# Four graph layers on one core: a ring of 1024 instead of 16384 bytes for Pool's DMA descriptors

## The reference

```python
h = jnp.maximum(_layernorm(x, axis=-1), 0.0)
x = x + _L0_gnn_ref(h, edge_attr_32, src, dst)       # mean of h[src] * pattern, plus h
h = jnp.maximum(_layernorm(x, axis=-1), 0.0)
x = x + _L1_gnn_ref(h, edge_index, Wq, Wk, Wv, Wo)   # attention over a node's edges
h = jnp.maximum(_layernorm(x, axis=-1), 0.0)
x = x + _L2_gnn_ref(h, W, src, dst)                  # sum of h[src], then @ W
h = jnp.maximum(_layernorm(x, axis=-1), 0.0)
x = x + _L3_gnn_ref(h, edge_index, sh0, sh1, sh2, W) # tensor products with edge attributes
```

## Time and profile before

| | |
|---|---|
| median of 3 runs | 16,172.44 us |
| runs | 16,150.69 to 16,204.41 us |
| span of the profiled execution (first to last instruction) | 14,816.7 us |
| busy: PE, POOL, DVE, ACT | 87%, 84%, 65%, 26% of the span |
| layer 0, layer 1, layer 2, layer 3 (about) | 74 to 3370, 3790 to 7280, 7530 to 10700, 10865 to 14660 us |
| DMAs that Pool issues | 9000 (L492), 294 + 98 (L509), 98 (L501), 98 (L471), 2 (L477, L482): 9590 |

### The profile page before, as it was taken

One profiled execution on the slowest core, in us unless ns is written; L12 is line 12 of the kernel. 1 busy time (PEld: TensorE's weight loads), 2 busy tenths in 40 slices (PEclk: granted clock), 3 DMA queues, 4 the chain that ended last, 5 costly groups with the idle time before them and its releaser, 6 DMA issues.

```text
span 14816.7 us, 226154 instructions
## 1 busy us (share of the span) xinstructions
PE 12890.3 (87%) x57644; PEld 10677.8 (72%) x57644; DVE 9612.6 (65%) x13223; ACT 3874.6 (26%) x4265; POOL 12431.7 (84%) x18594
## 2 busy tenths in 40 slices
PE   7999999992699999999689999999769999999996
PEld 6888888881577777777578888888756666767764
DVE  7666666664577777777666666666656665666665
ACT  2222222220233333333222222222211111111111
POOL 6888888887888888888778888888888888888884
PEclk9999999995899999999889999999989999999998
DMA  5444444442344444444345555545433333333332
GB/s 174 148 148 157 157 155 151 149 151 46 101 123 122 124 124 123 122 123 124 90 119 130 129 130 128 131 127 131 110 76 87 86 90 83 90 86 87 87 86 56
DMA packets 1340717, 1727.48 MB, mean 117 GB/s; under 512 B 501932, under 2 KB 1145566, under 8 KB 1339646
## 3 DMA queue, kind: packets, MB, share of 16 engines
q10 hardware_dynamic: 705956, 1154.87, 24.6%
q1 hardware_dynamic: 327194, 407.86, 9.6%
q0 software_dynamic: 306880, 158.96, 7.6%
HBM read 1140.23 MB, written 580.36 MB: 116 GB/s over the span
## 4 chain that ended last, share of the span: by engine, by line
POOL 41%; issue 32%; PE 20%; DVE 5%; POOLq 1%; DMA 0%; DVEq 0%; ACT 0%; ACTq 0%; SPq 0%
POOL rows L492 22%; POOL pace L497 16%; PE psum L690 12%; PE psum L773 7%; POOL outs L509 2%; PE psum L764 2%; DVE work L1340 1%; DVE work L1315 1%; POOLq L496 1%; POOL q_edges L471 1%; POOL work L501 1%; DVE tile_rows L924 0%; DVE work L1323 0%; DVE rows L931 0%; DVE outs L1347 0%
## 5 line engine op out<-in xcount | busy, mean ns | idle before, releaser
L690 PE MATMUL psum<-h_parts,one_hot 128*128 128x448 f32 x49406 | 10813.2, 377 | 482.0 <-ACT one_hot L539 262.4
L690 PEld LDWEIGHTS psum<-h_parts,one_hot 128*128 128x128 f32 x49406 | 9428.8, 192 | 1500.6 <-ACT one_hot L539 313.0
L492 POOL DMA_INDIRECT rows<-h_table,idx x9000 | 8662.9, 963 | 1966.9 <-POOL pace L497 1537.1
L546 ACT ACTIVATE one_hot<-keys 128x896 fp32r<-128x896 bf16 x2533 | 2359.9, 950 | 6435.5 <-PE psum L690 4314.0
L497 POOL MEMSET pace<- 128x288 f32 x9000 | 3213.9, 357 | 18.1 <-issue 13.2
L924 DVE TENSOR_TENSOR tile_rows<-psum,h_mask 128x448 f32<-128x448 f32 x2722 | 1686.2, 619 | 1252.3 <-PE psum L690 991.3
L931 DVE TENSOR_REDUCE rows<-tile_rows 128x32 f32<-128x448 f32 x2722 | 1677.0, 616 | 58.9
L773 PE MATMUL psum<-work,bd_t 128*128 128x512 f32 (+1 forms) x3500 | 1359.2, 514 | 240.1 <-DVE work L1323 141.3
L1323 DVE TENSOR_TENSOR work<-psum,work 128x800 f32<-128x800 f32 x875 | 862.7, 988 | 920.9 <-PE psum L764 864.2
L773 PEld LDWEIGHTS psum<-work,bd_t 128*128 128x128 f32 x3500 | 654.9, 193 | 764.4 <-issue 443.4
L912 DVE TENSOR_REDUCE rows<-psum 128x32 f32<-128x448 f32 x807 | 503.1, 623 | 792.0 <-PE psum L690 741.7
(11 more groups left out here) (202 smaller groups left out, 6198.1 us busy)
## 6 DMA issues: line engine op xcount, KB each, us to landing
keys<-hots ACTq DMA_DIRECT2D x2542, 224.0 KB
keep_in<-keep_flat SPq DMA_DIRECT2D x2000, 100.0 KB
sums<-outs ACTq DMA_DIRECT2D x375, 400.0 KB
rows<-h_table,idx POOLq DMA_INDIRECT x9000
hots<-bit_hot ACTq DMA_DIRECT2D x506, 224.0 KB
hots<-work ACTq DMA_DIRECT2D x506, 224.0 KB
attn<-outs ACTq DMA_DIRECT2D x125, 800.0 KB
edge_in<-pattern_c SPq DMA_DIRECT2D x125, 400.0 KB
```

The costliest lines, as they stand in the source:

```text
L492: nc.gpsimd.indirect_dma_start(out=rows[:, r, j * D:(j + 1) * D], out_offset=None, in_=h_table[:, :], in_offset=bass.IndirectOffsetOnAxis( ...
L546: nc.scalar.activation(one_hots[i % LOOK[l]][:, :, :], loaded_hots[i % BIT_BUFS[l]], ACT.Copy).then_inc(one_hot_cast, 1)
L690: last = nc.tensor.matmul(banks[TILE_BANKS[l][b]][:, 0:H0 * D], one_hots[hot][:, h1, :], h_parts[:, part, h1 * H0 * D:(h1 + 1) * H0 * D], ...
```

## The change

```diff
 PE_COLS = ((8, 8, 8, 8, 8), (7, 7, 6, 6, 6), (8, 8, 8, 8, 8), (6, 6, 5, 5, 6))
 PACE = 288
+RING_BYTES = 1024
 PE_MAX = max(max(c) for c in PE_COLS)
...
     n = inputs["x"].shape[0]
-    nc = bacc.Bacc("TRN2", target_bir_lowering=False, num_devices=1)
+    nc = bacc.Bacc("TRN2", target_bir_lowering=False, num_devices=1, dynamic_dma_scratch_size=RING_BYTES)
```

## The result

The changed kernel takes 16,892.18 us (median of 3 runs, 16,885.69 to 16,894.46), the kernel before 16,172.44. The ratio is 1.0459, with a 95% interval of 1.0422 to 1.0497. The forecast of 16,179 missed by 713 us, and the time lies outside the range of 16,135 to 16,235 too. A run over 1.5% above the fastest of its kernel counts as slow and is left out of the ratios, though not of the medians: one of the kernel before at 16,333 us and one at 29,561 us.

The account below looks back on a forecast made before the run. Pool's gathers were taken to bound layers 0 and 2 and about half of layer 1, PE layer 3. 16,172.4 us plus 7.0 for the ring's end and 0 for its depth gave 16,179, range 16,135 to 16,235.

Parts of the forecast that it names:

- What bounds the kernel: Whole kernel: Pool's gathers set the pace in layers 0 and 2, about half of layer 1; PE in layer 3.
- 144 bytes a gather, seven in the ring: Descriptor ring: a gather takes 144 bytes of a partition, so 1,024 bytes hold 7.1 gathers, seven whole ones.
- Term 1: Pool passing the ring's end: 1,265 more passes of 9 ns, 11.4 us of Pool's time, 7.0 us on the path.
- Term 2: Depth of Pool's ring: eighth gather starts 10.3 us after the first, slowest landing takes 6.1 us; no wait, 0 us.
- Term 3: Tensor addresses: not numbered in the prediction; an effect of these or the part outside the span got 0.01 each way.
- The base of the sum: Whole kernel: runs take 16,172.4 us, 1,355.7 more than the profiled span; that part was taken as unchanged.
- Rival A: At the ring's end Pool waits for everything in flight: 788 passes of 1.0 us, 16,970 us; chance 0.04.
- Rival B: Only three or four gathers fit, so layer 0's 25 stores hold Pool up: about 16,260 us; chance 0.07.
- Rival C: Smaller ring makes layer 0's gathers as fast as layer 2's: 102 us would go, 16,075 us; chance 0.04.

Follow-up runs that it names:

- pad_1024: Changed kernel (ring of 1,024 bytes) plus 15,360 unused bytes a partition, so tensors keep their old addresses; 16,934.8 us, 1.1419 of the kernel before.
- the split by four: Changed kernel with each chunk's gathers telling two semaphores, four in turn on each; 16,210.0 us (1.0088 of before), on another chip 15,305.3 us (1.0011).

## Why the prediction was wrong

**What bounds the kernel** was right for the profiled execution, except that layer 3 counted as covered. Its cover was some 0.1 ms; with 506 us of stops Pool is the bound there as well, 448 us.

**144 bytes a gather, seven in the ring** was right: the first stop is the eighth gather, and with 2,048 and 2,560 bytes the 15th and the 18th.

**Term 1, the ring's end**, was right in its place: the gathers of 0.96 us stand seven apart (8997.72 and 9010.98 us in the timeline), and in layer 2 292 of 2,125 gathers take 956 ns or more, where the end every 7.1 makes 299; before it was 36. Its size is not shown. The gathers are 13 us busier, and 11 had been worked out, but the seven profiles with 1,024 bytes lie between 8,634 and 8,683 us and the four with 16,384 between 8,630 and 8,664. Either way it is small beside 2,074 us.

**Term 2, the depth, is the step that failed**: it was put at 0 us, and the stops come to 2,208. It failed in two sentences. "A gather's slots can be written again once it has landed" is not what the runs show: in this kernel they are taken back when the newest gather on the chunk's semaphore has landed. And "That slots are taken again costs nothing by itself", with the proof that the kernel before fills its ring at the 114th gather and keeps its 1.47 us. The observation is right, the inference isn't. A ring of 113.8 gathers is longer than any chunk's 20, so whenever it is full, it holds several semaphores, and by the rule above the landing that is waited for lies more than 80 us back. The kernel before never meets the case that the changed one meets twice a chunk: a full ring with one semaphore in it. The 10.3 us that I held against the slowest landing of 6.1 us were the distance to the oldest gather; the one that counts is the newest, 1.47 us back. With the right rule, the landing of 2.4 us and the 0.84 us behind it, a stop is about 2.4 + 0.84 - 1.47 = 1.8 us, and two in each of 500 chunks 1.8 ms. Measured were 2.2: 2.8 us a stop at 7, 1.6 at 14. The difference lies in the landing: in layers 0, 2 and 3 gather 6 lands 3.5, 4.1 and 3.0 us after its start on average, gather 13 2.1, 2.3 and 2.1. In layers 0 and 2 of the kernel before number 6 is as late (3.5 and 3.7); beside which transfers it runs I did not follow up.

The sentence of the Trainium skill that I set aside (Perfetto Trace Analysis, DMA Instruction, SWDGE) speaks of descriptors that don't fit in the buffer, and I had read it for one instruction. It tells when the DMA engines may start; that Pool is then tied to the transfer was my inference. The runs show Pool tied to its transfers though one instruction fills a seventh of the ring: what must fit are the DMAs issued one behind the other on one semaphore.

**Term 3, addresses**: 0, as taken; shown by pad_1024.

**The base of the sum** was wrong by itself: "1,355.7 more than the span; no view covers that part". No run here has such a part: wherever both are on record, time and span differ by 1.8 to 4.3 us (16,892.2 and 16,890.4, say). The profiled execution was then shorter than the three runs: it is like the 14,834 and 14,810 us of two chips here, while they are like the 16,054 us of another. No profile of one of the three runs shows which chain they had. The same change is 1.046, 1.105 or, with the addresses kept, 1.142 of before, by chip.

**Rival A** had the nature of the loss, waiting for what is in flight, and its 16,970 lies near the 16,892. That is chance: it puts 788 passes of 1.0 us on top of 16,172. By passes it would have been every 7.1 DMAs for any semaphore, which the split by four excludes; there are 1,000 stops of 2.2 us, from a base of 14,817. I gave it 0.04, since "the kernel before passes the end too", the same inference as above. **Rival B** is out: seven fit, and the stops don't follow layer 0's stores. **Rival C** is out: the gathers of layer 0 still take 997 ns. Why they are slower than those of layer 2 was not tested.

## What to carry to other kernels

A ring for Pool's descriptors must hold more DMAs than are issued one behind the other on one semaphore; 4,096 bytes did for 20 gathers of 144 bytes, and below that the newest DMA's whole latency is paid each time the ring fills. Where the ring must be small, let the DMAs tell two semaphores in stretches of about half the ring (here four gathers of seven). A resource that shows no price while it is oversized says nothing about its price when small: ask which situation (here, all entries of one semaphore) the old trace can't contain, and check that the profiled execution is as long as the timed runs before a sum is built on it.

## What was not expected of the hardware

- A DMA that finds the ring full does not wait for its oldest entry but for the newest DMA of a semaphore, and starts no sooner than 0.82 us after that landing with 1,024 bytes (medians at the stops 0.9 to 1.2 us), 0.92 with 2,048 and 0.95 with 2,560. Why it takes longer with the longer rings is open.
- The kernel before differs by 9% between executions on different chips (14,810 to 16,172 us), the changed one, with the padded one beside it, by 0.3% (16,886 to 16,943). In the changed one Pool and its gaps are 98% of the chain; in the other Pool and PE alternate.
- PE's own work grew by 553 us with the same 57,644 matmuls (12,890 to 13,443 us). It sat idle more ahead of its main line (482 us before, 1,337 in the changed kernel), and the mean granted clock, between full speed of 2.4 GHz and half, was 0.948 before and 0.891 after. None of it is on the chain that ended last.
